# A fused attention and mixture-of-experts kernel: every engine's order of work up to expert step 42 rearranged, and the first load of combine weights issued alone

## The reference

```python
x = x + xattn(layernorm(x), ctx, ctx, mask, ...)
x = x + moe(layernorm(x), ...)
```

## Time and profile before

| | |
|---|---|
| median of 3 runs | 298.83 us (298.77 to 298.99) |
| the profiled execution | 299.21 us |
| its span, first to last instruction | 297.4 us |
| instructions | 4503 |
| busy share PE, PEld, DVE, ACT, POOL | 96%, 70%, 60%, 54%, 61% |
| mean granted clock of TensorE | 0.998 |
| read from HBM, written | 27.54 MB, 1.18 MB |

### The profile page before, as it was taken

How to read it: one execution, slowest core, us unless ns; L and a number is a source line. 1 busy time by engine, 2 the same in 40 slices (tenths; PEclk the granted TensorE clock), 3 DMA queues, 4 the chain that set the end, 5 groups by cost and what they waited for, 6 DMA issues and landing times.

```text
span 297.4 us, 4503 instructions
## 1 busy us (share of the span) xinstructions
PE 284.9 (96%) x1427; PEld 206.9 (70%) x1427; DVE 179.6 (60%) x476; ACT 161.7 (54%) x298; POOL 182.9 (61%) x167
## 2 busy tenths in 40 slices
PE   2999999999999999999799999999999999999995
PEld 2756568757786787866666766767668888888882
DVE  0747855656755686796173427358965756566561
ACT  2555857574776677863342544573254564545541
POOL 2148686855576466342566966846706787877881
PEclk9999999999999999999999999999999999999999
DMA  6799300003000001101752432320045246334101
GB/s 210 244 361 297 128 0 3 0 2 100 7 2 0 3 1 57 51 0 45 264 185 82 141 124 90 129 83 3 1 151 193 90 141 210 116 100 142 71 2 71
DMA packets 9575, 29.01 MB, mean 98 GB/s; under 512 B 1232, under 2 KB 2256, under 8 KB 9424
## 3 DMA queue, kind: packets, MB, share of 16 engines
q1 hardware_dynamic: 8688, 27.15, 27.2%
q10 hardware_dynamic: 864, 1.57, 1.6%
HBM read 27.54 MB, written 1.18 MB: 97 GB/s over the span
## 4 chain that ended last, share of the span: by engine, by line
PE 86%; DVE 5%; DMA 4%; POOL 2%; issue 2%; ACT 0%; DVEq 0%; POOLq 0%
PE bank L1494 15%; PE bank L1495 15%; PE bank L1496 15%; PE bank L1573 10%; PE bank L1700 9%; PE bank L1561 6%; PE bank L1533 5%; PE bank L1542 3%; PE bank L1595 2%; PE bank L1602 2%; DMA k_T<-comb_dram 2%; POOL k_T L497 2%; DMA ctx_all<-in_ctx_in 1%; PE bank L1624 1%; DMA comb_dram<-comb_T 1%
## 5 line engine op out<-in xcount | busy, mean ns | idle before, releaser
L497 POOL TENSOR_TENSOR k_T<-x_T,k_T 128x512 f32<-128x512 f32 x64 | 94.0, 1475 | 44.8 <-DVE x_T L1274 34.7
L789 ACT ACTIVATE x_T<-bank 128x512 f32<-128x512 f32 x72 | 42.9, 597 | 68.4 <-PE bank L1496 68.3
L1274 DVE TENSOR_TENSOR x_T<-bank,x_T 128x512 f32<-128x512 f32 x64 | 44.1, 690 | 53.2 <-ACT x_T L789 29.5
L1494 PE MATMUL bank<-mT_hi,we_hi 128*128 128x512 f32 x144 | 62.5, 434 | 0.0
L1495 PE MATMUL bank<-mT_lo,we_hi 128*128 128x512 f32 x144 | 56.9, 395 | 0.0
L1496 PE MATMUL bank<-mT_hi,we_lo 128*128 128x512 f32 x144 | 56.8, 395 | 0.0
L1700 PE MATMUL bank<-k_T,w_in 128*128 128x512 f32 x78 | 36.6, 595 | 1.8 <-POOL k_T L497 1.8
L1494 PEld LDWEIGHTS bank<-mT_hi,we_hi 128*128 128x128 f32 x144 | 27.1, 188 | 9.1 <-issue 3.5
L1495 PEld LDWEIGHTS bank<-mT_lo,we_hi 128*128 128x128 f32 x144 | 27.1, 188 | 8.2 <-issue 2.9
L1573 PEld LDWEIGHTS bank<-vo,o_T 128*128 128x128 f32 x256 | 30.2, 192 | 2.3 <-issue 2.0
L1496 PEld LDWEIGHTS bank<-mT_hi,we_lo 128*128 128x128 f32 x144 | 27.0, 188 | 6.5
(11 more groups left out here) (127 smaller groups left out, 488.1 us busy)
## 6 DMA issues: line engine op xcount, KB each, us to landing
k_T<-comb_dram SPq DMA_DIRECT2D x32, 512.0 KB, 3.7
w_in<-in_w_gu SPq DMA_DIRECT2D x3, 768.0 KB, 4.4
w_in<-in_w_dn SPq DMA_DIRECT2D x1, 1152.0 KB, 9.7
w_in<-in_w_attn ACTq DMA_DIRECT2D x4, 256.0 KB, 4.8
w_in<-in_w_attn SPq DMA_DIRECT2D x2, 512.0 KB, 7.5
ctx_swap<-in_ctx_in SPq DMA_DIRECT2D x2, 384.0 KB, 12.0
out_x<-ctx_all SPq DMA_DIRECT2D x3, 256.0 KB, 4.6
x_all<-in_x SPq DMA_DIRECT2D x2, 256.0 KB, 5.7
```

Of the source, the lines that this page charges most:

```text
L497: pool.tensor_tensor(act[n % 4], s_u[n % 2], comb[u % RING][:, c % 2 * CW:(c % 2 + 1) * CW], ALU.mult).then_inc(weighed_ready, 1)
L789: a.activation(silu[n % 2], h_bank[n % 2][:], ACT.Silu).then_inc(silu_ready, 1)
L1274: v.tensor_tensor(into, u_bank[n % 2][:], silu[n % 2], ALU.mult).then_inc(s_u_ready, 1)
L1494: pe.matmul(dst, w_hi, m_hi, start=start, stop=False)
```

## The change

SyncE gets one wait: before load 1 is issued, load 0 must have landed. Loads 1, 2, 3 and all that follow on SyncE's queue stand behind it. The second half has no such wait.

```diff
                 for u in range(b * NE, (b + 1) * NE):
+                    if u == 1:
+                        sp.wait_ge(comb_loaded[0], 16)
                     load_weights(u)
```

TensorE:

```diff
             key(0, 7)
+            fold(1, 0)
             turn_ctx(1)
-            fold(1, 0)
+            fold(1, 1)
 
             scores(0)
...
             attend(14)
+            turn_xm(1)
             up(1)
-            project(13)
-            turn_xm(1)
             route(1)
...
             project(15)
+            down(0)
+            down(1)
             ffn_up(2, 0)
-            down(0)
+            up(4)
             ffn_up(2, 1)
-            down(1)
             down(2)
             ffn_down(2)
-            up(4)
+            turn_combine(0)
             up(5)
-            turn_combine(0)
             turn_x1(3)
...
             up(8)
             up(9)
-            up(10)
             down(5)
             down(6)
+            up(10)
...
-            down(28)
+            up(30)
             up(31)
             up(32)
             up(33)
             up(34)
-            up(35)
+            down(28)
             down(29)
             down(30)
             down(31)
             down(32)
+            turn_combine(1)
+            up(35)
             up(36)
             up(37)
-            turn_combine(1)
             down(33)
```

VectorE:

```diff
             keep_experts(0)
+            combine(0)
             gate_up(3)
-            combine(0)
             add_ffn(2)
             take_combine(0)
...
             gate_up(28)
+            keep_groups(1)
             gate_up(29)
             gate_up(30)
-            keep_groups(1)
             gate_up(31)
             gate_up(32)
+            keep_experts(1)
+            combine(1)
             gate_up(33)
-            keep_experts(1)
             gate_up(34)
             mT_low(3)
             gate_up(35)
-            combine(1)
             gate_up(36)
-            take_combine(1)
             act_low(36)
             gate_up(37)
+            take_combine(1)
```

ScalarE:

```diff
             spread(15)
+            normalise(3, 1)
             heads_out(14, 0)
-            heads_out(14, 1)
-            normalise(3, 1)
-            gate(1)
             take_xm(1)
             mT_high(1)
+            heads_out(14, 1)
+            gate(1)
...
+            gate(3)
+            split_hi(6)
             turn_x1(2)
...
             hidden(3, 1)
+            normalise(2, 2)
             gate(6)
...
+            dn_high(3)
+            dn_high(4)
             gate(18)
```

More of the change, by code:

```diff
@@ L610, in _ @@
             dn_low(2)
+            dn_low(3)
             weigh(21)
@@ L614, in _ @@
             weigh(23)
+            split_lo(7)
             weigh(24)
-            split_lo(7)
             weigh(25)
@@ L619, in _ @@
             weigh(27)
+            split_lo(8)
             weigh(28)
-            split_lo(8)
             weigh(29)
             weigh(30)
+            dn_low(4)
             weigh(31)
@@ L631, in _ @@
             weigh(41)
[L632 to L661, removed]
+            for n in range(42, N):
                 if weighted(n):
@@ L882, in _ @@
             spread(5)
+            split_hi(1)
             normalise(1, 0)
+            heads_out(5, 0)
+            turn_x1(0)
+            spread(6)
+            key(3, 0)
+            heads_out(5, 1)
+            hidden(0, 0)
             exponent(8)
[L886 to L889, removed]
+            exponent(9)
+            hidden(0, 1)
+            heads_out(6, 1)
+            spread(7)
             key(3, 1)
-            exponent(9)
@@ L893, in _ @@
-            hidden(0, 0)
-            spread(6)
+            spread(8)
+            heads_out(6, 0)
+            split_hi(2)
+            exponent(10)
             key(3, 2)
[L896 to L901, removed]
+            key(3, 3)
+            spread(9)
             heads_out(7, 0)
-            spread(8)
-            key(3, 3)
+            heads_out(7, 1)
             key(3, 4)
-            exponent(11)
@@ L927, in _ @@
-            spread(11)
-            exponent(12)
+            key(3, 5)
+            heads_out(8, 0)
+            key(3, 6)
+            key(3, 7)
+            heads_out(8, 1)
+            normalise(3, 0)
+            spread(10)
+            heads_out(9, 1)
+            take_xm(0)
+            split_hi(3)
+            heads_out(9, 0)
+            normalise(1, 1)
+            exponent(11)
+            exponent(12)
+            heads_out(10, 0)
+            heads_out(10, 1)
+            turn_x1(1)
@@ L958, in _ @@
             normalise(1, 2)
+            heads_out(15, 1)
             heads_out(15, 0)
-            heads_out(15, 1)
             gate(2)
+            gate(3)
+            split_hi(6)
             turn_x1(2)
             hidden(2, 0)
-            gate(3)
             dn_high(1)
+            dn_high(2)
             hidden(2, 1)
-            split_hi(6)
+            gate(4)
             normalise(1, 3)
-            gate(4)
             turn_x1(3)
+            hidden(3, 0)
             gate(5)
-            hidden(3, 0)
@@ L982, in _ @@
             gate(13)
-            dn_high(2)
+            normalise(3, 2)
             gate(14)
+            split_hi(7)
             gate(15)
@@ L987, in _ @@
             gate(17)
-            normalise(3, 2)
+            dn_high(3)
+            dn_high(4)
             gate(18)
-            take_xm(2)
             gate(19)
             gate(20)
+            take_xm(2)
+            mT_high(2)
+            normalise(2, 3)
             gate(21)
-            normalise(2, 3)
             gate(22)
-            dn_high(3)
-            split_hi(7)
             gate(23)
-            mT_high(2)
             gate(24)
+            gate(25)
             normalise(3, 3)
-            gate(25)
+            take_xm(3)
+            split_hi(8)
             gate(26)
-            take_xm(3)
-            mT_high(3)
             gate(27)
@@ L1888, in _ @@
             up(19)
+            up(20)
             down(14)
-            turn_xm(2)
             down(15)
             down(16)
-            up(20)
+            route(2)
+            down(17)
             up(21)
             up(22)
-            route(2)
-            down(17)
             down(18)
```

280 lines of the change are left out of this document (130 added, 150 removed).

## The result

The changed kernel took 296.49 us (median of six executions, 296.13 to 297.14) beside 298.77 for the kernel before on the same chip; a seventh execution of the changed kernel took 1308 us and is left out. That is a ratio of 0.9938, 95% interval 0.9923 to 0.9953, 1.9 us less by the ratio and 2.3 by the medians of that series. Measured again (experiment 6) it gave 0.9936 (0.9923 to 0.9948). Forecast were 3.0 us and a time of 295.8; 296.5 lies within the range of 295.0 to 298.0, on the side forecast.

A forecast was written before the change was run, and what follows sets the result against it. TensorE was taken to bound the kernel, so only its waits could go: -0.7 - 1.7 - 0.6 = -3.0 us, from 298.8 to 295.8 us, with a range of 295.0 to 298.0.

The forecast's parts named there:

- weigh(4), -1.7: First routing half: combine weights loaded earlier, so TensorE's wait at down(4) for GpSimd's weighing goes, 1.7 us less.
- the work itself: TensorE's 281 pieces are the same in both orders; changed borders between kinds taken as 0, between -0.3 and +0.3 us.
- The bound: TensorE, busy 284.9 of 297.4 us; a new order can bring its few waits and little more.
- costed at nothing: Folds, turn_ctx(1), weight splits, keys' softmax and other moved pieces stay covered by slack: 0, keeping 0 to +2.5 us.
- xm_T, -0.7: At route(1): up(1) now stands between turn_xm(1) and route(1) and hides ScalarE's copy, 0.7 us less.
- The cause inside that term: First load of the first routing half lands in 3.7 us alone, against 5.0 with three loads right behind it.
- rival (a): First load gains nothing by going alone, still takes 5.0 us; TensorE waits 1.1 us: 296.9 us, chance 0.13.
- Later loads, 0.2 at worst: Loads behind the added wait on SyncE go out later; weigh(6) delays down(6) by 0.2 us at worst.
- comb_w, -0.6: Second routing half: combine(1) ends before TensorE reaches turn_combine(1), so its wait goes, 0.6 us less.
- Rival (b): Attention stage no longer dense; new waits of 0.5 us each give back 1.5 to 3.0: 297.3 to 298.8, chance 0.13.
- (c): Second half's comb_w late for the earlier turn_combine(1), TensorE waits 4.8 us: 300.6 us, slower, chance 0.14.
- (d): Waits only move elsewhere on TensorE, needing 3 us of new waits: 298.8 us, chance 0.05.

The follow-up runs named there:

- experiment 6: The changed kernel, unchanged, measured and profiled a second time: 296.74 us, ratio 0.9936.
- experiment 3: The changed kernel with turn_xm(1) put back behind up(1), directly ahead of route(1): 297.91 us, ratio 0.9987.
- experiment 5: The kernel before, unchanged, profiled a second time: 298.29 us, ratio 0.9996.
- experiment 9: Repeat of the changed kernel without the added wait on SyncE: 296.58 us, ratio 0.9940.
- experiment 1: The changed kernel without the added wait on SyncE, first measurement: 296.92 us, ratio 0.9953.
- experiment 4: The changed kernel with combine(1) on VectorE moved behind gate_up(33), gate_up(34) and mT_low(3): 299.65 us, ratio 1.0056.
- experiment 2: The kernel before with only the added wait on SyncE, order untouched: 298.64 us, ratio 1.001.
- experiment 10: The changed kernel with a wait ahead of each of loads 1, 2 and 3, so loads 0 to 3 go singly: 296.60 us, ratio 0.9942.

## Why the prediction was right, and where it was not

The direction and the place held: three waits of TensorE were taken away and no new one came. Two terms were mis-sized, the largest one (weigh(4), -1.7) and the work itself (0), and the cause given inside the largest was wrong. By its steps:

- **The bound.** Right. All that changed is in TensorE's idle time and its borders.
- **The work itself, 0 (between -0.3 and +0.3).** Mis-sized. Up to route(1) the pieces that both orders hold take 0.81 us less at turn_xm(1), and yet route(1) starts only 0.2 earlier. In the first pair of profiles the other pieces add some 0.6 us: turn_ctx +0.3, project +0.3, turn_probs +0.2, fold +0.2, route +0.1, less 0.5 at the keys (leaving out a 0.4 that only passed from key(3, 2) to ffn_up(0, 0)). Each piece changes by 0.1 to 0.3 where its neighbours are others; that the neighbours are the reason is read from the profiles, no experiment took them apart, and for fold(1, 1) the landing of its weights can have a share. I had seen borders of 0 to 0.1 and taken them to cancel. up(31) adds 0.4 further on: gate_up(29) now stands behind keep_groups(1), whose eight operations ran from 196.2 to 199.5. That is one cover that failed, of those "costed at nothing", well inside the +2.5 that was kept.
- **xm_T, -0.7.** Right as a wait (0.86 in experiment 3), but most of it was given back by the borders ahead of it.
- **weigh(4), -1.7.** The steps were right: load at 138.2 (138.07), weigh(4) 142.0 to 143.3 (141.5 to 142.8), TensorE at 143.5 (143.88), with 1.1 us left over and not 0.2. The term failed in its first line, where the load of 5.0 us and the wait of 1.8 us were taken for the kernel's own. They were that execution's. In experiment 5 the wait is 0.3 as shown, 0.4 by the starts of the pieces. Against the first profile the term is -1.9, against the second -0.4. No run put the first routing half's order back, so this size is read from profiles alone. The median of the runs of before lies between the two profiled times, and its wait probably does too; how often the fetch meets load 0 in an unprofiled run, no run can say.
- **The cause inside that term.** Also wrong. I took 3.7 alone against 5.0 in company. Alone, at this place, the first load took 3.3 to 4.0 us in eight profiles; in company 3.8, 3.8, 3.9 and 4.2 in four, beside the 5.0. So company costs a first load some 0.2 us in the mean, with ranges that overlap, and the order alone leaves room for that, if only 0.06 us in experiment 9: there and in experiment 1 down(4) has no wait. That is what rival (a) said of the mechanism, and the rule of the Trainium skill named there (DMA: Bandwidth & Descriptors, "Two DMAs through the same engine are not ordered") agrees with the fifteen parts at 3.84. Its time was wrong, because it kept the 5.0. The fixed cost of about 2 us that the prediction takes from the Trainium skill (DMA: Bandwidth & Descriptors, "Anatomy of one DMA") stands there for DMAs that GpSimd issues; the loads here go out on SyncE, and no run here splits a load into such parts.
- **Later loads, 0.2 at worst.** Right. Load 1 was issued at 141.4 and landed at 145.0; weigh(6) ended at 146.5, down(6) started at 148.4.
- **comb_w, -0.6.** Right, 0.7 by starts. combine(1) ended at 208.0 for 208.7 forecast, TensorE came at 209.55 for 209.2.
- **Rival (b)** fell: 99.90 of the 100 us from 17 to 117 are busy. **(c)** was not reached, by 1.6 us, and is what experiment 4 made of it. **(d)** fell: it needed 3 us of new waits, and there are none.

The sum again, with the sizes found: xm_T -0.8, comb_w -0.7, borders +0.6, up(31) +0.4, and weigh(4) -1.9 in the first profile, which gives -2.4 (spans: -2.7), or -0.4 in the second, which gives -0.9 (up(42): 225.07 to 223.82, -1.25). The measured -1.9 lies between.

What else separates two executions is the start: scores(0) stood at 18.9 to 19.8 us in the profiles with the changed folds, and at 18.1 to 18.8 in those of the order of before. Part of that is the fold that now stands ahead of scores(0); the rest is the landing of weights and the length of key(0, 0), which the change does not touch, and waits for key_room. The start can be left out: both orders have done the same pieces when key(1, 3) starts, at 23 to 24 us, and again when up(42) starts.

| from the start of key(1, 3) to that of up(42) | us |
|---|---|
| order of before: first profile, experiment 5 | 203.22, 201.70 |
| order of before with the added wait: experiment 2 | 202.21 |
| changed order: first profile, experiment 6 | 200.44, 200.52 |
| changed order with no added wait: experiments 1, 9 | 200.44, 200.48 |
| changed order with three waits: experiment 10 | 200.39 |

The five profiles of the changed order lie within 0.13 us, whatever the waits on SyncE. Against them the kernel before took 1.2 us more in one profile and 2.8 in the other. That the forecast of 3.0 came near the 2.7 of the first pair of profiles is in part luck: terms that were left out (+1.0 for borders and up(31)) were covered by a wait of 1.8 that other executions don't have. The profile from which all was read was at the slow end of the kernel's executions (299.21 us, where nearly all lie from 297.5 to 299.1), and with a term of 0.4 in place of 1.7 the same sum would have been -1.7, and less with the left-out terms.

## What to carry to other kernels

A wait in one profiled execution is not yet the kernel's. Before a term is built on a landing that is longer than its like, look whether all parts of the transfer were late or only the last one, and what else the DMA queues carried in that window; a second profile of the unchanged kernel costs little and here would have given the largest term as 0.4 beside 1.7. And where a reordering takes waits of a few tenths, the borders between kinds of work are terms of the same size: count them piece by piece, also where the pieces are the same.

## What the runs showed of the hardware that I had not expected

- A single 16 KB packet of instructions on the DMA engines took 0.9 to 1.5 us in 154 of the 156 cases in thirteen profiles. The two others ran early in a load of 512 KB and took 1.94 us (the first profile) and 2.10 us (experiment 2, at 176.93 us); one of the load's sixteen parts landed 1.2 and 1.6 us behind the other fifteen, and the loads took 5.0 and 5.2 us. In eight of the nine other profiles where a fetch came during load 0 it started less than 0.8 us before the landing, in the ninth 1.0 us, and those landings took 3.3 to 4.0.
- Four loads of 512 KB issued together landed later one after the other (in experiment 9 4.2, 5.1, 7.3 and 8.0 us), while the first was hardly slowed: 3.8 to 4.2 against 3.3 to 4.0 alone. Of the 7.3 and 8.0 the last 1.1 are again one late part beside a fetch; the first four loads of the second half there, which met no fetch, took 3.9, 4.8, 5.6 and 6.3. Issued one behind the other, they took 3.7, 3.7, 3.7 and 4.1.
- On VectorE L1172 took 1.38 us, L1171, of the same size, 0.28; L1209 took 1.10 in the changed kernel and 0.39 in experiment 4. A weighing on GpSimd ran beside the long ones (from 196.35 for 1.27 us, and from 206.42 for 1.30 us), and none beside L1209 in experiment 4, at 212.38. L1217 in the earlier trace rows had GpSimd beside it too, from 200.93 on.
